# Attention values parked in device memory, one gather for keys and values

## The reference

```
# layer 1: relational attention, per edge type r
e      = leaky_relu(Q_r[dst] . a_q + K_r[src] . a_k)
attn   = exp(e - segment_max(e, dst)) / segment_sum(exp(...), dst)   # within one type
h      = sum over r of segment_sum(V_r[src] * attn, dst);  x = x + elu(h)

# layer 2: transformer attention, 8 heads of 16 features
score  = sum_d(Q[dst] * (K[src] @ W_edge[type])) / 4 * mu[head, type]
w      = exp(score - segment_max(score, dst))
agg    = segment_sum(V[src] * w, dst) / (segment_sum(w, dst) + 1e-10)
```

## Time and profile before

| | |
|---|---|
| Median of 3 executions | 6560.58 us (6554.14 to 6580.65) |
| Profiled execution | 6499.4 us, its span 6497.7 us |
| Granted TensorE clock, mean | 0.656 |
| Busy: TensorE, its loads | 3728.7 us (57%), 3244.4 us (50%) |
| Busy: VectorE, ScalarE, GpSimd | 2938.5 us (45%), 822.6 us (13%), 3273.6 us (50%) |

### The profile page before, as it was taken

One profiled execution on the slowest core, in us unless ns is written; L12 is line 12 of the kernel. 1 busy time (PEld: TensorE's weight loads), 2 busy tenths in 40 slices (PEclk: granted clock), 3 DMA queues, 4 the chain that ended last, 5 costly groups with the idle time before them and its releaser, 6 DMA issues. The chain is left out here.

```text
span 6497.7 us, 81708 instructions
## 1 busy us (share of the span) xinstructions
PE 3728.7 (57%) x19254; PEld 3244.4 (50%) x19255; DVE 2938.5 (45%) x9185; ACT 822.6 (13%) x1860; POOL 3273.6 (50%) x3327
## 2 busy tenths in 40 slices
PE   0000889866666466653644443677775666546665
PEld 0000788855655355542624332466665566346664
DVE  5000666643433333333794434266673444343334
ACT  0000111120111011120100000111111111311112
POOL 4775555536664466603004663166665566036662
PEclk9999777765555555565555555855555666768887
DMA  5232444432222222223402222211111111111112
GB/s 187 74 77 76 118 113 113 116 61 62 66 64 51 60 64 65 64 48 102 112 3 56 68 67 34 73 41 40 41 35 39 41 42 42 11 43 52 53 52 34
DMA packets 394236, 415.69 MB, mean 64 GB/s; under 512 B 230871, under 2 KB 296473, under 8 KB 394137
## 3 DMA queue, kind: packets, MB, share of 16 engines
q0 software_dynamic: 105984, 211.53, 13.1%
q1 hardware_dynamic: 233240, 141.69, 7.8%
q10 hardware_dynamic: 54912, 61.36, 3.5%
HBM read 325.69 MB, written 88.62 MB: 64 GB/s over the span
## 5 line engine op out<-in xcount | busy, mean ns | idle before, releaser
L603 POOL DMA_INDIRECT ring<-table_gine,idx x1248 | 1220.5, 978 | 962.0 <-DVE mraw L641 407.8
L1518 PE MATMUL ps<-msg,oh 128*128 128x128 f32 (+2 forms) x4160 | 919.0, 389 | 476.8 <-DVE HA L641 425.2
L1518 PEld LDWEIGHTS ps<-msg,oh 128*128 128x128 f32 x4160 | 819.6, 289 | 544.4 <-DVE HA L641 419.9
L641 DVE TENSOR_TENSOR mraw<-ps,ring 128x512 f32<-128x512 f32 x520 | 358.4, 689 | 1076.2 <-remote 671.7
L641 DVE TENSOR_TENSOR HA<-HA,ps 128x128 f32 (+2 forms) x2080 | 598.3, 288 | 249.3 <-DVE HA L641 124.9
L622 POOL DMA_INDIRECT ring<-table_rel,idx x368 | 350.9, 954 | 628.4 <-PE ps L1663 458.7
L603 POOL DMA_INDIRECT ring<-table_keys,idx x416 | 459.2, 1104 | 406.2 <-SPq L184 202.4
L1527 PE MATMUL ps<-wt,ear 64*128 64x128 f32 x2496 | 599.4, 410 | 60.9 <-DMA ear<-edge_attr_T 44.0
L603 POOL DMA_INDIRECT ring<-table_msg,idx x416 | 399.7, 961 | 464.4 <-SPq L184 215.9
L1527 PEld LDWEIGHTS ps<-wt,ear 64*128 64x128 f32 x2496 | 511.9, 300 | 130.0 <-issue 120.3
L603 POOL DMA_INDIRECT ring<-table_values,idx x416 | 400.3, 962 | 293.5 <-DVE msg L641 135.6
(11 more groups left out here) (288 smaller groups left out, 6103.1 us busy)
## 6 DMA issues: line engine op xcount, KB each, us to landing
ear<-edge_attr_T SPq DMA_DIRECT2D x312, 128.0 KB
oh<-slot_rows ACTq DMA_DIRECT2D x104, 256.0 KB
slot_records<-msg SPq DMA_DIRECT2D x32, 650.0 KB, 11.2
arena<-slot_records SPq DMA_DIRECT2D x104, 200.0 KB
edge_attr_T<-arena ACTq DMA_DIRECT2D x104, 192.0 KB
ring<-table_gine,idx POOLq DMA_INDIRECT x1248
ear<-slot_rows ACTq DMA_DIRECT2D x104, 128.0 KB
arena<-in_edge_attr SPq DMA_DIRECT2D x50, 250.0 KB
```

The costliest lines, as they stand in the source:

```text
L603: pool.indirect_dma_start(out=ring[:, k % 4, j, 0:width], out_offset=None, in_=table[:, :], in_offset=bass.IndirectOffsetOnAxis(ap=idx[:, ...
L641: return V.tensor_tensor(o, x, y, op)
L1518: ins = M.matmul(out_of(t, j), oh[:, t.s4, j, :], x, start=True, stop=True)
```

## The change

Value rows of both attentions go through a new tensor in device memory, `slot_values`, one contiguous 256 KB block a batch in slot order.

Layer 1: GpSimd gathers all 104 batches one after another into a ring of 12 batches in the space of `HA`, from the moment the table is written; SyncE stores each batch to `slot_values`. In the relational loop ScalarE's queue loads each batch back with one plain DMA. VectorE makes plain one-hots (one instruction a batch), and ScalarE multiplies them by the weights, one 128x128 instruction a tile.

Layer 2: keys and values stand beside each other in one table, `table_keys_values`, 1024 bytes a row, with 5 rows a node; the values are written five times. Pass A gathers these rows, and SyncE stores the value halves to `slot_values`; a slot of the ring is free when the scores are made and the store has landed. Pass B gathers nothing. SyncE loads the values back. The turned one-hots are compared from target rows that ScalarE's queue loads, the maxima are looked up as three bf16 parts that VectorE sums, and messages and weights are summed in PSUM over all batches, by two matmuls a tile, with a first and a last group of 7 matmuls over zeros.

```diff
-PRE = 12
+DEEP = 12
...
-        tab2k = dram("table_keys", [NPAD * NREL, D])
-        tab2v = dram("table_values", [NPAD, D])
+        vals = dram("slot_values", [NB, P, B * D])
+        tab2 = dram("table_keys_values", [NPAD * NREL, 2 * D])
...
+            for k in range(NB):
+                sp.wait_ge(qa.gath[k % 4], 16 * B * (k // 4 + 1))
+                if k >= 4:
+                    sp.wait_ge(values_out[k % 4], 16 * (k // 4))
+                sp.dma_start(vals[k], vdeep[:, k % DEEP].rearrange("p j d -> p (j d)")).then_inc(values_out[k % 4], 16)
...
+            t2b = tab2.rearrange("(b p r) (w d) -> b p r w d", p=P, r=NREL, w=2)
+            for b in range(NBLK):
+                sp.wait_ge(pn_free, QV_EVACS + b + 1)
+                sp.dma_start(t2b[b][:, :, 1, :], T3[4][:, b, :].unsqueeze(1).to_broadcast([P, NREL, D])).then_inc(t_out, 16)
...
+                sp.dma_start(t2v[b][:, :, 0, :], kwb[:, b % 2]).then_inc(keys_out[b % 2], 16)
...
-            table(tab2v, T3[4], 4)
+            sp.wait_ge(t_out, 16 * (3 + NBLK))
+            join.to("tr_values")
+            for k in range(NB):
+                sp.wait_ge(qm.gath[k % 4], 16 * B * (k // 4 + 1))
+                sp.wait_ge(values_out[k % 4], 16 * (NB // 4 + k // 4))
+                sp.dma_start(vals[k].rearrange("p (j d) -> p j d", j=B), kvring[:, k % 4, :, D:2 * D]).then_inc(values_out[k % 4], 16)
+            join.to("tr_zero")
+            for k in range(NB):
+                sp.wait_ge(values_out[k % 4], 16 * (NB // 4 + k // 4 + 1))
+                if k >= 4:
+                    sp.wait_ge(qt["messages"], k - 3)
+                sp.dma_start(ring[:, k % 4, :, 0:D], vals[k].rearrange("p (j d) -> p j d", j=B)).then_inc(values_in[k % 4], 16)
...
             for k in range(NB):
-                if k >= PRE + 4:
-                    pool.wait_ge(qa["sums"], k - 3)
+                if k >= 4:
+                    pool.wait_ge(qa.gath[k % 4], 16 * B * (k // 4))
+                if k >= DEEP:
+                    pool.wait_ge(values_out[k % 4], 16 * ((k - DEEP) // 4 + 1))
+                    pool.indirect_dma_start(
+                        out=vdeep[:, k % DEEP, j, :], out_offset=None, in_=tab1[:, :],
+                        in_offset=bass.IndirectOffsetOnAxis(ap=idx5[:, k * B + j:k * B + j + 1], axis=0)).then_inc(qa.gath[k % 4], 16)
...
+            for k in range(NB):
+                if k >= 4:
+                    pool.wait_ge(qm["scores"], k - 3)
+                    pool.wait_ge(values_out[k % 4], 16 * (NB // 4 + k // 4))
+                for j in range(B):
+                    pool.indirect_dma_start(
+                        out=kvring[:, k % 4, j, :], out_offset=None, in_=tab2[:, :],
+                        in_offset=bass.IndirectOffsetOnAxis(ap=idx5[:, k * B + j:k * B + j + 1], axis=0)).then_inc(qm.gath[k % 4], 16)
...
-            def weighted_onehots(t):
+            def weights(t):
                 dve.wait_ge(qa["exp"], t.n + 1)
-                w = small[:, t.s4, 0:B]
-                tt(w, small4[:, t.s4, B:2 * B], small3[:, t.s4, 1:2 * B:2], ALU.mult).then_inc(weight_set, 1)
-                yield
                 if t.late(4):
-                    dve.wait_ge(qa["sums"], t.n - 3)
-                for j in range(B):
-                    ins = V.tensor_scalar(oh[:, t.s4, j, :], iota_n[:, :], dl[:, bass.ds(t.k * B + j, 1)], w[:, j:j + 1],
-                                          ALU.is_equal, ALU.mult)
-                ins.then_inc(qa["onehot"], 1)
-            run(dve, [(5, weighted_onehots), (3, logits), (1, dst_onehots)])
+                    dve.wait_ge(qa["onehot"], t.n - 3)
+                tt(small[:, t.s4, 0:B], small4[:, t.s4, B:2 * B], small3[:, t.s4, 1:2 * B:2], ALU.mult).then_inc(weight_set, 1)
+            run(dve, [(5, weights), (4, onehots(qa["plain"], qa["sums"], oh)), (3, logits), (1, dst_onehots)])
...
-            join.to("trA")
-            ch(V.memset(AG[:, :], 0.0))
+            split([MXP[:, :, i, :] for i in range(3)], MX[:, :, :], mx_rest)
             join.to("tr_zero")
...
+            def tr_dst_onehots(t):
+                t2 = Batch(t.r, t.s, 1)
+                dve.wait_ge(drin[t.s4], t2.u * 16 + 16)
+                V.tensor_scalar(oT[:, t.h, 0], drow[:, t.s4], iota_p, None, ALU.is_equal).then_inc(qt["onehotT"], 1)
...
                     dve.wait_ge(qt["exp"], t.n - 3)
-                tt(small3[:, t.s4, 0:B * NHEAD], score[:, bass.ds(t.k * (B * NHEAD), B * NHEAD)],
-                   ps[:, 2 + t.h, 0:B * NHEAD], ALU.subtract).then_inc(qt["logits"], 1)
+                own = small4[:, t.s4, 0:B * NHEAD]
+                ch_tl.step(V.reduce_sum(own.rearrange("p (j g) -> p j g", j=B),
+                                        ps[:, 7, 0:B * 3 * NHEAD].rearrange("p (j i g) -> p j g i", j=B, i=3), AX))
+                yield
+                ch_tl.done()
+                dve.sem_inc(qt["picked"], 1)
+                ch_tl.done()
+                dve.sem_inc(qt["logits"], 1)
...
-                dve.wait_ge(qt.gath[t.s4], t.u * (16 * B) + 16 * B)
-                for j in range(B):
-                    ins = tt(msg[:, t.s4, j, 0:D].rearrange("p (g d) -> p g d", g=NHEAD),
-                             ring[:, t.s4, j, 0:D].rearrange("p (g d) -> p g d", g=NHEAD),
-                             msg[:, t.s4, j, D:W2N].unsqueeze(2).to_broadcast([P, NHEAD, HD]), ALU.mult)
-                ins.then_inc(qt["messages"], 1)
-            run(dve, [(5, acc_pair(qt, agg2, W2N)), (3, tr_message), (2, tr_logit), (0, onehots(qt["onehot"], qt["sums"], oh))])
-            dve.wait_ge(qt["acc"], NB * B)
-            join.to("trB")
-            den = agg2[:, :, D:W2N]
+                dve.wait_ge(values_in[t.s4], Batch(t.r, t.s, 1).u * 16 + 16)
+                tt(msg[:, t.s4, :, 0:D].rearrange("p j (g d) -> p j g d", g=NHEAD),
+                   ring[:, t.s4, :, 0:D].rearrange("p j (g d) -> p j g d", g=NHEAD),
+                   msg[:, t.s4, :, D:W2N].unsqueeze(3).to_broadcast([P, B, NHEAD, HD]), ALU.mult).then_inc(qt["messages"], 1)
+            run(dve, [(4, tr_message), (2, tr_logit), (1, tr_dst_onehots), (0, onehots(qt["onehot"], qt["sums"], oh))])
...
+            def values_back(t):
+                act.wait_ge(values_out[t.s4], t.u * 16 + 16)
+                if t.late(4):
+                    act.wait_ge(qa["sums"], t.n - 3)
+                act.dma_start(ring[:, t.s4, :, 0:D], vals[bass.ds(t.k, 1)].rearrange("a p (j d) -> p (a j) d", j=B)).then_inc(values_in[t.s4], 16)
+            def weighted_onehots(t):
+                act.wait_ge(qa["plain"], t.n + 1)
+                act.wait_ge(weight_set, t.n + 1)
+                for j in range(B):
+                    ins = A.activation(oh[:, t.s4, j, :], oh[:, t.s4, j, :], ACT.Copy, scale=small[:, t.s4, j:j + 1])
+                ins.then_inc(qa["onehot"], 1)
+            run(act, [(6, weighted_onehots), (4, att_exp), (0, att_in), (4, values_back)])
...
-            run(act, [(2, tr_exp), (0, onehotT(qt, lambda t: t.n))])
+            def tr_rows_in(t):
+                if t.late(4):
+                    act.wait_ge(qt["onehotT"], t.n - 3)
+                act.dma_start(drow[:, t.s4], slotrow[1:2, bass.ds(t.k * B, B), :].rearrange("w t s -> w (t s)")
+                              .to_broadcast([P, B * P])).then_inc(drin[t.s4], 16)
+            run(act, [(3, tr_exp), (0, tr_rows_in)])
...
+                pe.wait_ge(values_in[t.s4], t.u * 16 + 16)
                 blocks = blocks_of(pe, PE, t)
                 for j in range(B):
                     ins = M.matmul(psf[:, bass.ds(blocks[j] * D, D)], oh[:, t.s4, j, :],
-                                   vpre[:, t.k, j, :] if early else ring[:, t.s4, j, 0:D], start=False, stop=False)
+                                   ring[:, t.s4, j, 0:D], start=False, stop=False)
                 ins.then_inc(qa["sums"], 1)
-            run(pe, [(6, att_sums), (2, att_lookups)], lead=PRE // 4 + 2)
...
-            run(pe, [(4, sums(qt, W2N, pair(W2N), ready="messages")),
-                     (1, node_rows(qt, rows_at(MX, NHEAD), lambda t, j: ps[:, 2 + t.h, j * NHEAD:(j + 1) * NHEAD], own, "logits")),
-                     (0, turn_onehot(qt, own))])
+            for z in range(7):
+                n = min(512, NPAD + NBLK * NHEAD - z * 512)
+                M.matmul(ps[:, z, 0:n], b2row[0:1, :], wt[0:1, 0:n], start=True, stop=False)
+            def tr_lookups(t):
...
+                for j in range(B):
+                    ins = M.matmul(ps[:, 7, j * 3 * NHEAD:(j + 1) * 3 * NHEAD], oT[:, t.h, 0, j * P:(j + 1) * P],
+                                   MXP[:, bass.ds(blocks[j], 1), :, :].rearrange("p a i g -> p (a i g)"), start=True, stop=True)
+                ins.then_inc(qt["node"], 1)
...
+            def tr_into(t):
+                pe.wait_ge(qt["onehot"], t.n + 1)
+                pe.wait_ge(qt["messages"], t.n + 1)
+                for j in range(B):
```

(51 more changed lines are left out.)

47 lines of the change are left out of this document (23 added, 24 removed).

## The result

The changed kernel takes 6727.89 us (6720.76 to 6738.25, 4 runs), the kernel before 6562.81 on the same chip: a ratio of 1.0249, interval 1.0224 to 1.0275. It is slower, where 6290 was forecast and 6520 was the upper end. The profiled execution took 6729.7 us, span 6727.9. All later runs fell on other chips, and there the sign turned: 0.9929 (0.9913 to 0.9946), a gain of 0.7%. Both have to be explained.

The account below looks back on a forecast made before the run. No engine was over 57% busy; GpSimd's gathers bound the relational loop, and TensorE's signals came late beside gathers. Terms -259 + 210 + 0 + 20 - 240 = -269 gave 6230 us profiled, 6292 as a median; range 6070 to 6520.

Parts of the forecast that it names:

- Relational loop, -259: Layer 1's relational loop: without gathers 2.79 us a batch, TensorE next to bound, 563 to 304 us.
- the floor of 5.0: Relational loop before the change: four gathers of 1.25 us make at least 5.0 us a batch; it runs at 5.1.
- Lookups beside the gathers, +210: Layer 1's lookups and segment work: late signals beside 416 gathers lose 195 of 434 us, plus 15 for the start.
- rival A: Layer 1's lookups: the freeze lasts as long as GpSimd issues, +415 for +210, 6496 us in all; 22%.
- the upper bound of 415: Layer 1's lookups: about 12 batches beside the gathers, the other 86 at 2.02 us, ending near 3640 instead of 3225.
- The argument from 4760 to 4832 us: Pass A before the change: 48 gathers without a stop, VectorE still busy 50.91 of 72 us, suggesting a milder lookup cost.
- Pass B, -240: Layer 2's pass B: gathers and late releases go, TensorE bounds, 415 us against 655; bounds -344 and -172.
- The 3.7 us a turn: Pass B: TensorE's time a batch, taken between 2.7 us at the high clock and 4.36 at the low.
- the bound of 4.36 us: Pass B at the low clock: relational turn of 2.79 plus 1.57 us for sums of 8 columns; gives -172.
- Tables, 0: Layer 2's table stores: five value writes stay hidden beside the matmuls, no cost; bounds -7 and +30.
- Pass A, +20: Layer 2's pass A: a ring slot also waits for its value store, mostly done by then; bounds 0 and +50.
- Rival C: Pass A: wide gathers slow with their bytes; 1 us a gather makes +147, 6708 us; 10%.

Follow-up runs that it names:

- the second chip: Kernel before and changed kernel, both unchanged, run again on another chip: 5681.76 us before, 5644.98 us changed, ratio 0.9929.
- the open ring: Changed kernel with VectorE's messages of pass B made one turn earlier (lag 3 for 4): 5463.21 us, 0.9589 to the kernel before; on another chip 5460.65, 0.9600.
- work behind the signal: Changed kernel with four short matmuls behind the signalling matmul of each batch of lookups: 5638.92, 5645.44 and 5643.72 us (0.9901, 0.9916, 0.9914).
- pauses: Changed kernel where GpSimd waits for each batch of layer 1's gathers to land before issuing the next: 5738.04 and 5737.27 us (1.0075, 1.0078).

## Why the prediction was wrong

*Relational loop, -259.* It came to -262, at 2.8 us a batch. Right in size, and GpSimd is gone as the bound. TensorE is not alone in its place: it was busy 224 of 294 us and waited 44 us for ScalarE's weighted one-hots, which the prediction had taken to fit. The reading of the loop before was off as well: 530 us by 104 gives 5.1, but the gathers that wait are 88 batches, from 3471.7 to 3982.7 us, 5.8 each; the floor of 5.0 is met on the second chip, and the 0.8 between are time lost on the first.

*Lookups beside the gathers, +210.* It came to +473, with 10 more for a first gather at 2953.9. This is the step that failed first. That signals come late was seen in the earlier trace rows, and rival A named it; I priced it with the relational loop of the earlier trace rows, where GpSimd pauses between batches, instead of the place with the same structure, back-to-back gathers beside the same lookups. Rows 3 also hid its size: the first steps there, 31 and 43 us, are a delay that is still growing, to 86 us with two batches under way. Even the upper bound of 415 was too low: the gathers took 1.34 us each, not 1.25, and ended at 3512 (48 us), the last signals took another 25, and the lookups left to do numbered 89, not 86. The argument from 4760 to 4832 us in the earlier trace rows did not carry over.

*Pass B, -240.* It came to -50, outside its own bounds. I added up TensorE's work and never asked what is queued behind VectorE's wait for the sums, which is the question that finds the ring. The 3.7 us a turn forecast for TensorE agrees with the 3.8 measured once the ring was open, but by luck: it was taken between the levels for a clock over 0.61, and the clock stayed at 0.50. What hid that is the bound of 4.36 us, the sum at the low level, which was too high: it carried the gaps of the relational turn of the earlier trace rows, which the open ring hides.

*Tables, 0.* -1 between the last sum and pass A. *Pass A, +20.* +46, inside the bounds. It is +13 where signals are in time, so some 30 of it are late signals: ScalarE's remote waits at the turned scores went from 190.6 to 303.6 us. Rival C is out: a gather of 1024 bytes took GpSimd 1060 ns against 1104 in the earlier trace rows, and on the second chip 1206 against 1171. Those of layer 1 took 1016 against 954, although VectorE was busy for only 24 of 558 us beside them; so gathers get slower without VectorE's instructions too. What makes the 150 ns between the two loops of the earlier trace rows, which the prediction put down to those instructions, stays open.

```profile
L654 POOL DMA_INDIRECT arena<-table_keys_values,idx x416 | 440.9, 1060 | 1164.4 <-SPq L186 896.0 <-DVEq L1179 153.7 <-issue 114.0
L645 POOL DMA_INDIRECT HA<-table_rel,idx x416 | 422.5, 1016 | 293.5 <-DMA table_rel<-arena 158.1 <-issue 135.3
```

The sum: the lookups missed by 273, pass B by 190, pass A by 26, the rest by 10. From the forecast of 6292 the miss of the lookups alone leads to 6565, the same as the kernel before (6563), that of pass B alone to 6482: neither alone gives the sign, both together do. (The chances had a slip too: the parts named for "faster" add up to 0.845, not 0.82.) By the same account a kernel with the open ring would stand near 6540 on the first chip, the same as before; that is worked out, not measured.

Left open: why TensorE's signals come late on one chip of six, and what lets them through. Each chip was visited once, so it isn't shown either that the chip is the cause and not a state that it was in at the time. The kernel before lost there too: 6563 against 5681 to 5695 us. Both pointers, work behind the signal and pauses, could not be tried where they would tell.

## What to carry to other kernels

Price a stall by the place with the same structure, not by the loop with the nearest name: here the same late signal left a loop whose gathers wait for it at 5.8 us a batch for 5.0, and one beside gathers that wait for nothing at 44.8 for 2.0. Match a waiting instruction to its signal by counting batches, not by the nearest end before it. For each loop write down the ring of waits through every engine and ask of each wait what stands behind it on its engine; adding up the busiest engine's work finds no closed ring, and moving one stage by one turn opened this one for 3.3%. Before a change is judged by one chip, run both kernels on a second one.

## What was not expected of the hardware

Between chips one and the same kernel differed by 15% (6563 and 5682 us), with waits named remote as the mark of the slower one. Late signals came only beside indirect DMAs and for up to 25 us behind the last of them. In the frozen stretch they were 86 us late, in which GpSimd issued about 64 gathers (86 by 1.34). Within a long run of gathers a group of slower ones comes back, with single ones up to 2.6 us on the first chip and 7.0 on the second; it comes in the frozen stretch too, where VectorE is busy for 24 of 558 us.

TensorE busy 389.58 of 390 us with these f32 matmuls was granted 0.50, while four bf16 matmuls more a batch took the lookups, 62% busy, from 0.55 to 0.83.
